# Moving the query-key products, the causal selects and one key convolution in a delta-rule decoder layer

## The reference

```python
qkv = silu(conv1d(layernorm(x) @ Wqkv))        # causal, 4 taps per channel
q, k = l2norm(q), l2norm(k)
def step(M, inp):                              # per token, M is [128, 128] per head
    M = M * exp(g_t)
    Mk = einsum('bhd,bhdv->bhv', k_t, M)
    M = M + einsum('bhd,bhv->bhdv', k_t, (v_t - Mk) * b_t)
    o_t = einsum('bhd,bhdv->bhv', q_t, M)
```

## Time and profile before

| | |
|---|---|
| median of 3 runs | 2021.34 us (2016.12 to 2033.63) |
| profiled execution | 2010.82 us, span 2008.8 us |
| mean granted PE clock | 0.967 |
| busy PE, DVE, ACT, POOL | 1898.0, 1128.0, 933.2, 742.4 us |

### The profile page before, as it was taken

How to read it: one execution, slowest core, us unless ns; L and a number is a source line. 1 busy time by engine, 2 the same in 40 slices (tenths; PEclk the granted TensorE clock), 3 DMA queues, 4 the chain that set the end, 5 groups by cost and what they waited for, 6 DMA issues and landing times.

```text
span 2008.8 us, 45498 instructions
## 1 busy us (share of the span) xinstructions
PE 1898.0 (94%) x16962; PEld 1549.8 (77%) x16962; DVE 1128.0 (56%) x2048; ACT 933.2 (46%) x2987; POOL 742.4 (37%) x1143
## 2 busy tenths in 40 slices
PE   5899999999999999999999999999997799999999
PEld 4688888887878888888888888888887565656574
DVE  6756566566657475655657574756554352524333
ACT  2556464646455555646465654556463221213121
POOL 1345363635355454536264544545362000000000
PEclk9899899999999899989999998999897899999999
DMA  3011111201011111111020111111114503121100
GB/s 118 7 32 41 25 35 31 43 23 38 22 39 32 33 40 25 35 25 40 26 43 23 38 29 37 30 35 35 25 28 147 157 22 94 43 84 52 64 20 21
DMA packets 220197, 87.11 MB, mean 43 GB/s; under 512 B 138320, under 2 KB 204240, under 8 KB 219280
## 3 DMA queue, kind: packets, MB, share of 16 engines
q1 hardware_dynamic: 220048, 84.83, 16.7%
HBM read 57.28 MB, written 27.53 MB: 42 GB/s over the span
## 4 chain that ended last, share of the span: by engine, by line
PE 50%; issue 24%; POOL 9%; DVE 7%; ACT 4%; DMA 4%; SPq 1%; POOLq 1%; DVEq 0%; ACTq 0%
PE bank L555 18%; PE bank L864 4%; PE bank L814 3%; DVE vT L1376 2%; PE bank L823 2%; PE bank L776 2%; POOL blkT L1785 2%; POOL prod L1781 2%; PE bank L765 2%; PE bank L684 2%; PE bank L808 2%; ACT vv L1077 2%; PE bank L830 1%; PE bank L927 1%; PE bank L945 1%
## 5 line engine op out<-in xcount | busy, mean ns | idle before, releaser
L555 PE MATMUL bank<-x_hi,w_hi 128*128 128x512 f32 x1024 | 429.9, 420 | 14.7 <-DVE vT L1376 14.3
L555 PE MATMUL bank<-x_hi,w_lo 128*128 128x512 f32 x1024 | 408.4, 399 | 1.6 <-issue 1.6
L555 PE MATMUL bank<-x_lo,w_hi 128*128 128x512 f32 x1024 | 405.7, 396 | 0.0
L555 PEld LDWEIGHTS bank<-x_hi,w_hi 128*128 128x128 f32 x1024 | 196.3, 192 | 55.8 <-issue 13.4
L555 PEld LDWEIGHTS bank<-x_hi,w_lo 128*128 128x128 f32 x1024 | 195.1, 191 | 45.2 <-issue 2.0
L555 PEld LDWEIGHTS bank<-x_lo,w_hi 128*128 128x128 f32 x1024 | 196.1, 192 | 31.9 <-issue 0.4
L1376 DVE SCALAR_TENSOR_TENSOR qT<-bank,cw,qT 128x511 f32<-128x511 f32 (+2 forms) x192 | 142.0, 747 | 51.0 <-ACT qT L1026 46.5
L1841 POOL TENSOR_TENSOR rstd<-ve,mhalf 128x1 f32<-128x1 f32 x32 | 17.4, 544 | 389.1 <-DVE ve L1600 389.1
L1209 ACT ACTIVATE o_tmp<-bank 128x128 f32<-128x128 f32 x256 | 67.4, 278 | 174.3 <-PE bank L830 174.3
L1376 DVE SCALAR_TENSOR_TENSOR vT<-bank,cw,vT 128x511 f32<-128x511 f32 (+2 forms) x192 | 143.0, 745 | 8.6 <-ACT vT L1026 4.1
L1376 DVE SCALAR_TENSOR_TENSOR kT<-bank,cw,kT 128x511 f32<-128x511 f32 (+2 forms) x192 | 143.4, 747 | 5.0
(11 more groups left out here) (221 smaller groups left out, 4424.4 us busy)
## 6 DMA issues: line engine op xcount, KB each, us to landing
w_raw<-in_w_heads SPq DMA_DIRECT2D x64, 256.0 KB, 2.8
o_d<-og SPq DMA_DIRECT2D x64, 256.0 KB, 2.6
o_raw<-o_d SPq DMA_DIRECT2D x16, 1024.0 KB, 6.1
x_in<-in_x SPq DMA_DIRECT2D x16, 256.0 KB, 3.7
blkN_d<-nT SPq DMA_DIRECT2D x64, 64.0 KB, 2.1
t<-blkT_d SPq DMA_DIRECT2D x64, 64.0 KB, 2.4
wo_raw<-in_w_out SPq DMA_DIRECT2D x4, 1024.0 KB, 9.2
x_res<-in_x SPq DMA_DIRECT2D x16, 256.0 KB, 2.7
```

The source lines that it names most:

```text
L555: last = mm(bank[bk][:, :], w[:, kind % 2, d, :], xx[:, d, b * S:(b + 1) * S], start=(n == 0), stop=(n == 3 * ND - 1))
```

## The change

The query-key products are made by batch, each group right behind the transposes of that batch's queries: `qk(0)` after Z1, `qk(1)` after Z2, `qk(2)` before Z3, `qk(3)` after Z3. Groups have the same eight instructions as before. `probabilities` goes by batch too; on DVE, the first stands ahead of the last query convolution, the others ahead of the wait for `t32`. POOL's four selects stand ahead of the substitution. DVE's convolution of K0, and the tap of it on ACT, stand ahead of the joins' small copies. `JOIN_FILL` has 8 products where `qk(2)` and `qk(3)` were (2 before), and six of the places in `FILL` have 8 where they had 9. Nothing is computed more or less often.

```diff
--- before.py
+++ after.py
@@ -61,8 +61,8 @@
 AHEAD = 7
 JOB_BANK = [{Q_: (0, 3, 0, 3)[b], Z_: 1}.get(kind, job % 2) for job, (kind, b) in enumerate(JOBS)]
 
-FILL = ((0, 6), (9, 9), (9, 9), (9, 9))
-JOIN_FILL = (7, 2, 2, 1)
+FILL = ((0, 6), (8, 8), (8, 8), (8, 8))
+JOIN_FILL = (7, 8, 2, 1)
 HALVES = 2
 EARLY, LATE = slice(0, P // 2), slice(P // 2, P)
 FRONT = [slice(2 * j * PAIR, 2 * j * PAIR + PAIR) for j in range(2)]
@@ -675,13 +675,14 @@
                         proj(*JOBS[job], JOB_BANK[job], n, n + 1)
                     part[0] += count
 
-                def qk(c):
-                    if c == 0:
-                        pe.wait_ge(silu_done, 12 * h + 12)
+                def qk(b):
+
+                    pe.wait_ge(silu_done, 12 * h + conv_index(Q_, b) + 1)
+                    if b == 0:
                         pe.wait_ge(nT_done, 4 * h + 4)
-                    pe.wait_ge(pT_done, 4 * h + max(c - 1, 0))
-                    for b in range(B):
-                        last = mm(grid(5 + 2 * (c % 2))[:, b, :], kT[:, b, c, :], qT[:, b, c, :], start=True, stop=True)
+                    pe.wait_ge(pT_done, 4 * h + max(b - 1, 0))
+                    for c in range(NC):
+                        last = mm(grid(5 + 2 * (b % 2))[:, c, :], kT[:, b, c, :], qT[:, b, c, :], start=True, stop=True)
                     last.then_inc(qk_mm, 1)
 
                 pe.wait_ge(ktok_done, 4 * h + 3)
@@ -691,11 +692,13 @@
                     if job == NJ - 1:
                         ahead(3 * ND)
                         q_transpose(b - 1)
+                        qk(b - 1)
                     whole_job(h, job)
                     if kind == Z_:
                         v_transpose(b)
                         if b:
                             q_transpose(b if job == NJ - 1 else b - 1)
+                            qk(b if job == NJ - 1 else b - 1)
 
                 def join16_y():
 
@@ -777,13 +780,9 @@
                                       start=True, stop=True)
                     last.then_inc(z64_mm, 1)
 
-                qk(0)
-                qk(1)
                 join16_y()
                 ahead(JOIN_FILL[0])
                 join16_z()
-                qk(2)
-                qk(3)
                 ahead(JOIN_FILL[1])
                 join32_y(0)
                 ahead(JOIN_FILL[2])
@@ -1171,19 +1170,20 @@
                     act.wait_ge(z64_mm, 2 * h)
                     fn(y64[LATE, 2 * g:2 * g + 2, :, :], larges(half_bank(g), LATE), ACT.Copy).then_inc(y64_done, 1)
 
-                keep16_y()
                 if more:
+                    act.wait_ge(conv_done, 12 * h + 12)
                     for kind in (K_, V_, Q_):
                         taps_of(h + 1, kind)
-                    act.wait_ge(proj_done, NJ * h + NJ)
-                    split(h + 1, V_)
-                join16()
-                if more:
                     act.wait_ge(cw_ready, 3 * h + 6)
                     act.wait_ge(qk_mm, 4 * h + 4)
                     act.wait_ge(kg_done, 3 * h + 3)
                     act.wait_ge(vtr_done, 4 * h + 4)
                     tap(h + 1, K_, 0)
+                keep16_y()
+                if more:
+                    act.wait_ge(proj_done, NJ * h + NJ)
+                    split(h + 1, V_)
+                join16()
                 keep32_y(0)
                 keep32_y(1)
                 keep32_n(0)
@@ -1455,28 +1455,31 @@
 
                 if not first:
                     gated(h - 1, NC - 1)
+                def probabilities(b):
+
+                    dve.wait_ge(qk_mm, 4 * h + b + 1)
+                    if b == 0:
+                        dve.wait_ge(ke_done, 3 * h + 3)
+                        dve.wait_ge(masked, 4 * h + 4)
+                    tt(pT[:, b, :, :], grid(5 + 2 * (b % 2)), pT[:, b, :, :], ALU.mult).then_inc(pT_done, 1)
+
                 conv(h, V_, 3)
                 conv(h, Q_, 0)
                 conv(h, Q_, 1)
                 conv(h, Q_, 2)
+                probabilities(0)
                 if more:
                     split(h + 1, K_)
                 conv(h, Q_, 3)
-
-                def probabilities(c):
-
-                    dve.wait_ge(qk_mm, 4 * h + c + 1)
-                    if c == 0:
-                        dve.wait_ge(ke_done, 3 * h + 3)
-                        dve.wait_ge(nT_done, 4 * h + 4)
-                    dve.wait_ge(masked, 4 * h + c + 1)
-                    tt(pT[:, :, c, :], grid(5 + 2 * (c % 2)), pT[:, :, c, :], ALU.mult).then_inc(pT_done, 1)
+                probabilities(1)
+                probabilities(2)
+                probabilities(3)
 
                 dve.wait_ge(t32_in, 64 * h + 64)
                 for c in range(NC):
                     nc.vector.transpose(tT[:, :, c, :], t32[:, :, c, :]).then_inc(tT_done, 1)
-                probabilities(0)
-                probabilities(1)
+                if more:
+                    conv(h + 1, K_, 0)
                 dve.wait_ge(z16_mm, h + 1)
                 for j in (0, 1):
                     t = TILES[j]
@@ -1487,8 +1490,6 @@
                 dve.wait_ge(z16_done, 2 * h + 2)
                 for c in range(NC):
                     nc.vector.transpose(t32[:, :, c, :], tT[:, :, c, :]).then_inc(t32_done, 1)
-                probabilities(2)
-                probabilities(3)
 
                 def join32(g):
                     dve.wait_ge(z32_mm, 2 * h + g + 1)
@@ -1504,8 +1505,6 @@
 
                 join32(0)
                 join32(1)
-                if more:
-                    conv(h + 1, K_, 0)
                 join64(0)
                 join64(1)
                 if more:
@@ -1769,6 +1768,12 @@
                 tt(k_norm[:, :, :], k_sqe[:, :, :], half[:, :].rearrange("p (b c) -> p b c", b=B), ALU.pow).then_inc(knorm_done, 1)
                 for c in range(NC - 1):
                     scaled_k(c)
+                pool.wait_ge(nT_done, 4 * h + 4)
+                pool.wait_ge(ke_done, 3 * h + 3)
+                hold(pool, "pool")
+                for c in range(NC):
+                    nc.gpsimd.affine_select(out=pT[:, :, c, :], in_=pT[:, :, c, :], compare_op=ALU.is_ge, fill=0.0, base=0,
+                                            pattern=[[0, B], [1, P]], channel_multiplier=-1).then_inc(masked, 1)
 
                 pool.wait_ge(inv_set, 2 * h + 2)
                 pool.wait_ge(blkN_in, 32 * h + 32)
@@ -1784,11 +1789,6 @@
                     rows = blkT[:, j + 1:BLK, 0:j + 1]
                     tt(rows, rows, products, ALU.subtract).then_inc(sub_step, 1)
 
-                pool.wait_ge(nT_done, 4 * h + 4)
-                hold(pool, "pool")
-                for c in range(NC):
-                    nc.gpsimd.affine_select(out=pT[:, :, c, :], in_=pT[:, :, c, :], compare_op=ALU.is_ge, fill=0.0, base=0,
-                                            pattern=[[0, B], [1, P]], channel_multiplier=-1).then_inc(masked, 1)
                 pool.wait_ge(gam_done, 4 * h + 4)
                 for c in range(1, NC):
                     tt(kdT[:, :, c - 1, :], kT[:, :, c, :], gam[:, :, c, :], ALU.mult).then_inc(kg_done, 1)
```

## The result

| | before | after |
|---|---|---|
| median | 2020.07 us (4 runs, 2016.12 to 2033.63) | 2078.26 us (4 runs, 2067.03 to 2088.45) |
| ratio | 1 | 1.0296 (95%: 1.0255 to 1.0337) |
| profiled execution, span | 2010.82, 2008.8 us | 2083.08, 2081.4 us |
| mean granted PE clock | 0.967 | 0.954 |

The change makes the kernel 3% slower: 58 us by the medians, against a forecast of 50. The two profiled executions are 72 us apart: that of before is faster than all four runs in the table, and that of after lies above its median.

The account below looks back on a forecast made before the run. PE, busy 94% of the span, was taken to bound the kernel with its pauses. Terms -6.3 + 16 + 4.5 + 36 = +50 us gave 2071 us on the median; forecast 2070 us, range 2030 to 2095.

Parts of the forecast that it names:

- Chunks, 36 us: In chunk 1, K3 and V0 start earlier and wait 1.4 and 1.0 us for DVE's convolutions, in fifteen heads: 36 us.
- rival (3): DVE's chain is faster than thought or fill order does not bind, so no chunk term: 2035 us; alone 0.05.
- The wait that comes at the first join, 16 us: At L712, PE waits 1.2 us instead of 0.24 for ACT's last query squares, in 16 heads: 16 us more.
- the one that goes, -6.3 us: At L712, PE arrives later, so nine waits for the DMA bringing inverted blocks shrink to 0.24 us each: 6.3 us gained.
- The joins, 4.5 us: Behind L723, eight fills do not fully cover DVE's negation and transposes; PE waits 0.3 us at L737, fifteen heads: 4.5 us.
- Hidden at no cost: Moved products wait for nothing; selects fit POOL's `blkN` wait; K0's convolution is hidden with half a microsecond to spare.
- The head at full clock, 93.0 us: Sign to check in the profile after: a head running at full clock should be 93.0 us long.
- Nothing on the clock: Likeliest case adds nothing for PE's clock; prediction is wrong if the mean granted clock moves by over 0.01.
- rival (2): The new pause ahead of L712 puts more heads at half clock, costing 20 us more: 2091 us; chance 0.15.
- Rival (1): Eight dense products behind the second join remove stops and clock drops, returning 42 us: 2029 us; chance 0.16.

Follow-up runs that it names:

- Experiment 2: The kernel before with only the fill numbers changed, six products moved from chunks 1 to 3 to chunk 0; 2050.97 us, ratio 1.0202.
- experiment 6: The changed kernel with the convolutions of K1 and K2, and their taps on ACT, one place earlier; 2046.32 us, ratio 1.0172.
- Experiment 4: The changed kernel with the last value transposes put ahead of job Z3 instead of behind it; 2068.77 us, ratio 1.0258.
- experiment 5: The kernel before with only POOL's four selects moved ahead of the substitution; 2021.02 us, ratio 1.0011.
- experiment 1: Query-key products, `probabilities` and selects as in the changed kernel; fills, tap and convolution of K0 as before; 2109.67 us, ratio 1.0466.
- experiment 3: The changed kernel with the fill numbers of before, K0's convolution staying ahead of the joins; 2111.67 us, ratio 1.0484.
- 7: The changed kernel with K1 and K2 convolutions one place earlier and the last value transposes ahead of job Z3; 2037.21 us, ratio 1.0139.
- 8: The kernel of 7 with four more fill products in the joins (7, 10, 3, 2) and fewer in the chunks; 2019.46 us, ratio 1.0028.
- 9: The kernel of 8 with its 22 join fills placed 10, 8, 2, 2, ten between the two 16-wide joins; 2023.78 us, ratio 1.0023.
- 10: The kernel of 8 with its 22 join fills placed 7, 8, 2, 1 and four ahead of the 64-wide joins; 2032.42 us, ratio 1.0074.

## Why the prediction was right, point by point

Forecast 2070 us, measured 2078: slower, by the mechanisms named, with the clock under-counted. The waits that I summed to 50 us came to 45 in the profile's list, and the clock, which I put at nothing, to some 15. The two errors partly cancel, so that the total came so near is in part luck.

*Chunks, 36 us.* Measured 29 us by the list of waits, and 34 us (2050.97 against 2017.01) as the cost of the fill numbers alone. One wait is 1.06 instead of 1.4 us and the other 0.85 instead of 1.0. Experiment 2 brings it about alone and experiment 6 takes it away, so rival (3) is out.

*The wait that comes at the first join, 16 us, and the one that goes, -6.3 us.* The new pause is 1.14 us, 18.2 us in 16 heads, where 1.2 was forecast, and the DMA no longer appears. With what else stands at that product, L712's 10.2 us became L715's 19.3: +9.1 us, forecast +9.7. Experiment 4 ties the pause to the value transpose.

*The joins, 4.5 us.* 6.7 us, 0.38 us in most heads instead of 0.3, with one of 2.4 us. That one (2.39 us, at 1591.19) is in the sixteenth head, which I had left out: it has no following head to take fills from, and the query-key products that covered DVE there are gone. The fifteen heads have 4.3 us.

*Hidden at no cost: the products' new place, the selects, K0's convolution.* Right: PE never waits at L685 in after, experiment 5 shows nothing, and experiments 1 and 3, which differ in the convolution's place, have the same time within 2 us (2109.67 and 2111.67). POOL's wait for `blkN` was to be 2.4 us shorter a head; over all heads it fell from 69.2 to 29.5 us, 2.5 us a head.

*The head at full clock, 93.0 us.* 92.6 and 93.3 us. But I had counted 3.7 us on top of before's shortest head; from the mean of its five at full clock it is 2.8 us. The smaller `kT` waits are 0.5 us of the difference.

*Nothing on the clock.* This step failed in part. I called the prediction wrong if the mean granted clock moved by over 0.01, and between the profiled executions it moved by 0.013: 58 us more at half clock. Between the medians of all executions (0.964 and 0.956) it moved by 0.008, some 38 us more at half.

The 41 executions of before give a price without any change to the kernel. Their clocks go from 0.955 to 0.969, and a straight line through their times rises by 0.38 us for each microsecond more at half clock. By it the clock's part between the medians is some 15 us. Experiment 1's net 0.27 gives 16 us for the profiled pair. I applied that price to the other kernels too. "Waits" are all idle time of PE at the lines L712, L723 and L737 (or what they are called there), unexplained stops included, and at L555 for `kT`, from the whole list, over before's 20.3 us:

| | waits | half clock x 0.27 | sum | fifteen heads |
|---|---|---|---|---|
| after | +45 | +16 | +61 | +70 |
| 2 | +29 | +4 | +33 | +38 |
| 3 | +42 | +50 | +92 | +97 |
| 4 | +41 | +13 | +54 | +61 |
| 6 | +19 | +17 | +36 | +32 |
| 7 | +16 | +8 | +24 | +18 |
| 8 | +9 | +2 | +11 | +3 |
| 9 | +11 | +8 | +19 | +12 |
| 10 | +13 | +1 | +14 | +7 |

The two together give the stretch within 10 us in every kernel. As a test of the price that is weak: only experiment 3 has much half-clock time, and it is nearly experiment 1, from which the price comes; in the others the clock's column is at most 17 us and the sum misses by up to 9. Of after's 70 us some two thirds are waits, and the clock has a quarter by this price; by PE's busy time, 28 us of the 70, it has at most two fifths. That part is rival (2), at about the 20 us that I gave it.

Its mechanism was half right. In six of after's fifteen heads a half-clock stretch begins within three microseconds of L715's start, behind the new pause, and in the fourth head one follows the stop of 2.08 us at L555 (before: the four heads with the longest waits for the DMA). Most of these are short and cheap: the twelfth head, with one, takes 93.3 us. The dear stretches begin 10 to 14 us behind L715, or six in one head: nine in after, six in before, each some 7 to 20 us long. Each of these fifteen begins within 2 us of an unexplained stop of 0.86 us or more (2.29 us at L756 in the fourth head). The reverse does not always hold: two such stops at L684 in before, 2.13 and 1.61 us, had no half clock behind them. So what brings the dear stretches is, as far as the traces show, these stops and not the new pause; no run took the stops away by themselves.

Where the stops fall is no accident of the small products. I numbered all that PE has in a trace (weight loads, matrix products and waits) in order of start. In the fifteen heads of the twelve kernels there are 256 unexplained stops of over 0.15 us (that there are as many as the distance is chance). In each kernel every one stands a whole multiple of 256 instructions behind the first, to within one. There are 114 or 115 such places in the fifteen heads, and 15 to 25 of them show a stop. Moving products changes which product stands at such a place: in the seventh head of after one falls on a fill product (2.14 us at L555), where in the kernel before the same place fell on L737 and passed without a stop. In all, after's heads have 19 such stops, 20.7 us, and before's 23, 17.2 us. Why more of after's are of the dear kind is open.

*Rival (1)*, that dense products behind the second join keep the clock up, is wrong in its size: the clock fell. Something of it is right, and I had not seen it. Without these products the clock falls in every head (experiments 1 and 3), so they don't raise it above before's but replace what the query-key products did there. On the unexplained stops the Trainium skill (Runtime: NRT & Kernel Launch, "Instruction fetch mechanics") says that code loading is hidden behind issue. If they are code loading, the traces do not agree with that. Their distance of 256 instructions is the block that the prediction cites, which speaks for it, though no row shows a load itself. They went from 14 to three at L728 with three more products ahead of them, as they would if those products gave the loading time; the other stops grew, and over the fifteen heads all of them together went from 21.8 to 18.9 us.

## What to carry to other kernels

Filler products are not free to move between places: when their starts are bound by another engine's steps, taking one out earlier moves the next start up into a wait, so count every start against what releases it (here 34 us for six products of 0.24 us each). When work is taken out from behind a step that other engines turn around, what it covered must be covered again; and a pause among small matrix products can cost more in clock than in waiting, so read the granted clock window by window, not its mean. Experiments 6 to 8 show the way to mend such a change: move the releasing steps on the other engines by as many places as the work moved, and then use the room for more cover where it is missing. Here that brought the kernel back to the time of before, and not below it.

## What the runs showed of the hardware

A pause of 1.75 us ahead of a run of 32-wide products was followed by half clock for some 17 us (windows of experiment 1), and it did so in nearly every head: a mean of 0.91 over fifteen heads, against 0.97 in the kernel without the pause. The pause of 1.14 us ahead of the 16-wide products, which after has too, left two of after's fifteen heads at full clock throughout.

A microsecond at half clock cost 0.38 us of time over 41 executions of the kernel before, and 0.27 us net in experiment 1, where PE's busy time rose by 0.38 us for each and its idle time elsewhere shrank.

In the fifteen heads of twelve kernels, PE made 256 stops of 0.15 to 2.9 us that no engine or DMA explains. All of them stand at places that are a whole multiple of 256 of its instructions apart, and none elsewhere.
